# The first cross attention's tiles as steps -16 to -1 of the local layers' pipeline, instead of a stage of its own with a loop

## What is computed

```python
xn = layernorm(x)                                   # 2048 rows of 128
q = xn @ Ly + Lo;  k = ctx @ Lx                     # per head
p = softmax((q @ k.T) / 8 + mask)
x = x + (p @ (ctx @ Tx) + To0) @ Ty + To1           # the first cross attention
y = layernorm(x)
for d in range(6):                                  # the local layers, on y
    y = y + local_attention(shifted(y), Wqkv[d], q_scale[d], k_scale[d]) @ Wo[d]
    y = y + gated_ffn(y, W1[d], W2[d])
x = x + y                                           # then three small cross attentions,
                                                    # an fp8 product and two expert layers
```

## Time and profile before

| | us |
|---|---|
| median of 3 runs | 2523.07 (2520.99 to 2523.55) |
| the profiled execution | 2521.31 |
| its span in the trace | 2519.5 |
| first mask (tile 0), and last mask (tile 15) of the cross stage | 22.27, 223.55 |
| first product of the local layers | 247.79 |
| first softmax of the local layers | 269.98 |
| TensorE busy | 2381.2 (95%) |
| VectorE, ScalarE, GpSimd busy | 1903.0, 1456.6, 1178.6 |

### The profile page before, as it was taken

How to read it: one execution, slowest core, us unless ns; L and a number is a source line. 1 busy time by engine, 2 the same in 40 slices (tenths; PEclk the granted TensorE clock), 3 DMA queues, 4 the chain that set the end, 5 groups by cost and what they waited for, 6 DMA issues and landing times.

```text
span 2519.5 us, 61076 instructions
## 1 busy us (share of the span) xinstructions
PE 2381.2 (95%) x25532; PEld 1440.2 (57%) x25532; DVE 1903.0 (76%) x3472; ACT 1456.6 (58%) x2048; POOL 1178.6 (47%) x867
## 2 busy tenths in 40 slices
PE   6887899999999999999999999988889999999999
PEld 5775556566665666666665666554555555455443
DVE  4765898999999899999999999966866766455222
ACT  2332566666666666666666666653467677566443
POOL 1222776777677767777767776741211111001000
PEclk9998999999999999999999999999899999999999
DMA  3000000000010000000000000002010101120110
GB/s 123 5 4 6 1 2 2 27 10 13 2 35 2 13 18 19 7 7 27 10 8 7 27 10 11 2 1 78 15 33 15 35 12 40 41 82 21 38 50 30
DMA packets 36006, 55.95 MB, mean 22 GB/s; under 512 B 6365, under 2 KB 20710, under 8 KB 35498
## 3 DMA queue, kind: packets, MB, share of 16 engines
q1 hardware_dynamic: 35754, 52.33, 6.6%
HBM read 51.13 MB, written 1.19 MB: 21 GB/s over the span
## 4 chain that ended last, share of the span: by engine, by line
PE 53%; DVE 23%; ACT 11%; issue 9%; POOL 2%; SPq 0%; DMA 0%; DVEq 0%; POOLq 0%; ACTq 0%
PE w L1417 9%; PE w L1407 9%; DVE turned L1057 4%; PE w L766 4%; DVE norm L1064 4%; PE w L791 4%; PE w L779 4%; PE py L804 4%; PE w L519 3%; DVE straight_odd L1052 2%; DVE top L568 2%; PE w L857 2%; ACT sq L1003 2%; ACT sq L994 2%; PE w L1536 2%
## 5 line engine op out<-in xcount | busy, mean ns | idle before, releaser
L593 POOL TENSOR_TENSOR prob<-prob,rden 128x1024 f32<-128x1024 f32 x112 | 213.4, 1905 | 206.3 <-DVE rden L582 206.3
L563 ACT ACTIVATE prob<-logit 128x512 f32<-128x512 f32 x224 | 137.9, 632 | 282.1 <-DVE logit L571 282.1
L1407 PE MATMUL w<-qT,m_fc 128*128 128x512 f32 x544 | 268.7, 606 | 0.4 <-ACT turned L1654 0.4
L1173 POOL TENSOR_TENSOR straight_odd<-straight_odd,turned 128x1024 f32<-128x1024 f32 x96 | 227.5, 2370 | 82.8 <-DVE turned L1057 79.8
L1173 POOL TENSOR_TENSOR straight<-straight,turned 128x1024 f32<-128x1024 f32 x96 | 226.6, 2369 | 43.5 <-DVE turned L1057 43.5
L1057 DVE TENSOR_TENSOR turned<-w,rot 128x512 f32<-128x512 f32 x384 | 245.6, 681 | 0.0
L1167 POOL TENSOR_TENSOR straight_odd<-straight_odd,rnorms 128x1024 f32<-128x1024 f32 x96 | 180.6, 1903 | 116.8 <-DVE rnorms L1078 116.8
L1064 DVE TENSOR_REDUCE norm<-sq 128x16 f32<-128x1024 f32 x192 | 224.3, 1210 | 0.0
L1167 POOL TENSOR_TENSOR straight<-straight,rnorms 128x1024 f32<-128x1024 f32 x96 | 180.6, 1901 | 72.4 <-DVE rnorms L1078 72.4
L766 PE MATMUL w<-b_wqkv,m_proj 128*128 128x512 f32 x384 | 192.0, 623 | 3.3 <-DVE turned L1057 2.0
L791 PE MATMUL w<-b_wqkv,m_proj 128*128 128x512 f32 x384 | 190.3, 618 | 0.0
(11 more groups left out here) (260 smaller groups left out, 5234.2 us busy)
## 6 DMA issues: line engine op xcount, KB each, us to landing
b_wqkv<-gates SPq DMA_DIRECT2D x64, 256.0 KB, 3.6
b_wqkv<-in_b_wqkv SPq DMA_DIRECT2D x18, 512.0 KB, 3.6
ctxT<-in_ctxT SPq DMA_DIRECT2D x64, 64.0 KB, 1.8
b_wo<-in_b_wo SPq DMA_DIRECT2D x6, 512.0 KB, 3.8
m_fc<-in_m_fc SPq DMA_DIRECT2D x1, 2304.0 KB, 8.8
m_proj<-in_m_proj SPq DMA_DIRECT2D x1, 2304.0 KB, 13.0
m_fc<-in_m_fc SPq DMA_DIRECT2D x8, 256.0 KB, 3.2
m_proj<-in_m_proj SPq DMA_DIRECT2D x8, 256.0 KB, 3.7
```

Of the source, the lines that this page charges most:

```text
L593: pool.tensor_tensor(flat, flat, k.rden[:, s, :, None].broadcast_to([P, HEADS, SEQ]), ALU.mult).then_inc(k.prob_ready, 1)
L1173: pool.tensor_tensor(k.straights[s][:, i, :, :], k.straights[s][:, i, :, :], k.turned[:, i, :, :], ALU.add).then_inc(added, 1)
L1407: pe.matmul(claim(("hidden", J, c)), k.m_fc[:, x, c * P:(c + 1) * P], k.m_xT[:, q, :], start=True, stop=True).then_inc(k.ring_full, 1)
```

## The change

The stage cross0 and its loop are gone. Its tiles are steps -16 to -1 of `layers_*`, all unrolled, in the three stages of a local step: step g computes queries and keys of tile g, values and scores of g-1, softmax and attention of g-2, and also the output products of g-3 (`cross_rows`, all eight in one piece, ahead of the softmax's transposes), the update of `k.x` for g-3 and the second normalisation of g-4. `oT` is written in two buffers in turn, so that line 661's successor (`output_bias`) waits for `o_psum` alone. The attention output of the cross tiles goes to `w2` instead of `w0`. The product with the row of ones is gone: GpSimd adds `a_to1`, spread over 128 partitions by its load, to `k.x` (`add_to1`) once the tile has been normalised. The quantisation jobs lie in steps -13 to -10, each on VectorE between the update and `output_bias`; `turn_x` of steps -11 and -10 waits for them, because they share `pt`. The rows are turned into `k.z` in steps -8, -4, 0 and 4.

The core of the diff:

```diff
-        k.a_to1 = sb("a_to1", [1, P])
+        k.a_to1 = sb("a_to1", [P, P])
+QUANTISE = -12
 def stages_of(g):
-    return [0 <= g - n < STEPS for n in range(3)]
+    return [-TILES <= g - n < STEPS for n in range(3)]
+def is_cross(g):
+    return -TILES <= g < 0
 def layers_tensor(pe, k):
+    def turn_x(g):
+        T = FIRST + g
+        pe.wait_ge(k.norm.normed, T + 1)
+        pe.wait_ge(k.xT_ready, T)
...
+        if g - 2 == QUANTISE:
+            pe.wait_ge(k.quant.done, 1)
+        pe.transpose(k.pt[:, 0:P], k.normed[:, g % 2, :], k.ident[:, :]).then_inc(k.xT_psum, 1)
...
+    def cross_scores(g):
+        T = FIRST + g
+        pe.wait_ge(k.qT_ready, T + 1)
+        if is_cross(g + 1):
+            pe.wait_ge(k.kT_ready, T + 2)
+        else:
+            pe.wait_ge(k.kT_ready, T + 1)
+            pe.wait_ge(k.k_turned, T + 2)
+        scores_tensor(pe, k, g % 2)
+    def cross_rows(g):
+        T = FIRST + g
+        pe.wait_ge(k.oT_ready, T + 1)
+        pe.wait_ge(k.updated, T)
+        for h in range(PAIRS):
+            mm = pe.matmul(k.py[:, 0:P], k.oT[:, h, g % 2, :], k.a_ty[:, h, :], start=(h == 0), stop=(h == PAIRS - 1))
+        mm.then_inc(k.y_psum, 1)
...
-    pe.wait_ge(k.quant.done, 1)
-    turn_in(0)
-    for g in range(STEPS + OUTPUT + 1):
+    turn_x(-TILES)
+    pe.wait_ge(k.loaded, 16 * N_URGENT)
+    for g in range(-TILES, STEPS + OUTPUT + 1):
+        if is_cross(g):
+            cross_queries(g)
...
+        if is_cross(g - 1):
+            cross_values(g - 1)
...
+        if is_cross(g):
+            cross_keys(g)
...
+        if is_cross(g - 3):
+            cross_rows(g - 3)
...
+        if is_cross(g + 1) and g >= -TILES:
+            turn_x(g + 1)
...
         if before2:
             turn_probs(g - 2, before)
...
+        if is_cross(g - 1):
+            cross_scores(g - 1)
...
         if before2:
             pe.wait_ge(k.pT_ready, FIRST + g - 1)
             attend_tensor(pe, k, g % 2, k.w2).then_inc(k.o_psum, 1)
 def layers_vector(dve, k):
+    def output_bias(g):
+        dve.wait_ge(k.o_psum, FIRST + g + 1)
+        dve.tensor_tensor(k.oT[:, :, g % 2, :], k.w2[:, :].rearrange("p (h n) -> p h n", n=P),
+                          k.a_to0[:, :, None].broadcast_to([P, PAIRS, P]), ALU.add).then_inc(k.oT_ready, 1)
...
+        if is_cross(g - 2):
+            cross_shift(g - 2)
...
+        if is_cross(g + 2):
+            cross_stats(g + 2)
+        if is_cross(g):
+            query_bias(g)
+        if is_cross(g + 2):
+            cross_normalise(g + 2)
+        if is_cross(g - 4):
+            cross_fresh(g - 4)
+        if before2:
             softmax_sum_vector(dve, k, T - 2, s)
...
+        if is_cross(g - 3):
+            cross_update(g - 3)
...
+        if g == QUANTISE + 1:
+            quantise_weights(dve, k)
+        if g == QUANTISE + 2:
+            fp8_weight_vector(dve, k)
+        if is_cross(g - 2):
+            output_bias(g - 2)
 def layers_gpsimd(pool, k):
+    def add_to1(g):
+        x = k.x[:, g + TILES, :]
+        pool.wait_ge(k.norm.normed, FIRST + g + 1)
+        pool.tensor_tensor(x, x, k.a_to1[:, :], ALU.add).then_inc(k.to1_added, 1)
```

More of the change, by code:

```diff
@@ L372, in _ @@
             gpsimd_program(nc, pool, k)
[L375 to L392, removed]
@@ L397, in cross0_tensor @@
[L397 to L452, removed]
-        if this:
-            pe.wait_ge(k.prob_ready, T + 1)
-            pe.wait_ge(k.v_ready, T + 2 if after else T + 1)
-            for h in range(PAIRS):
-                mm = pe.transpose(k.w2[:, h * P:(h + 1) * P],
-                                  k.prob[:, s, 2 * h:2 * h + 2, :].rearrange("p a m -> p (a m)"), k.ident[:, :])
-            mm.then_inc(k.pT_psum, 1)
-        if before:
-            rows(range(2, 6))
-        if this:
-            wait_apart(pe, k, k.pT_ready, T + 1)
-            pe.wait_ge(k.qT_ready, T + 2 if after else T + 1)
-            attend_tensor(pe, k, s, k.w0).then_inc(k.o_psum, 1)
-        if after2:
-            turn_x(T + 2, s)
-        if before:
-            rows(range(6, PAIRS))
-            pe.matmul(k.py[:, 0:P], k.ones[0:1, :], k.a_to1[0:1, :], start=False, stop=True).then_inc(k.y_psum, 1)
-    turn_x(first, 0)
-    turn_x(first + 1, 1)
-    pe.wait_ge(k.loaded, 16 * N_URGENT)
-    front(first, 0, False)
-    short_steps(pe, first, step)
@@ L935, in layers_tensor @@
             hidden(hid, 0, g)
-        if before:
+        if before and g >= 1:
             turn_queries(g - 1, this)
@@ L989, in layers_scalar @@
         if before2:
-            exp_scalar(act, k, T - 2, s, 8.0)
-        if this:
+            exp_scalar(act, k, T - 2, s, 0.125 if is_cross(g - 2) else 8.0)
+        if this and not is_cross(g):
             act.wait_ge(k.q_psum, T + 1)
@@ L1135, in layers_vector @@
             gate(hid, 0)
-        if this:
+        if local:
             rotate(g, 1, k.w1, k.k_turned, k.k_squared, k.kT_psum, k.k_added)
```

259 lines of the change are left out of this document (128 added, 131 removed).

## The result

The changed kernel takes 2527.72 us (median of 10 runs, 2521.92 to 2530.55) against 2522.82 for the kernel before (10 runs, 2520.99 to 2524.64): ratio 1.0019, 95% interval 1.0010 to 1.0027. It is a little slower, by 4.9 us where 11 were forecast. The same kernel, run again beside experiments, gave 2526.05 (11 runs) against 2522.89, ratio 1.0012 (1.0003 to 1.0021).

A forecast was written before the change was run, and what follows sets the result against it. It took a closed chain of 13.28 us a tile through VectorE, GpSimd, TensorE and ScalarE as the bound. At the full clock -8.2, plus 20 for the falling clock, on 2521.3 gave 2533, median 2534 us; 8-in-10 range 2512 to 2546.

The forecast's parts named there:

- The main case: Cross steps up to the first local softmax: slower by the longer chain and a falling clock, 2534 us, chance 0.57.
- the price of a fall of the clock, "I take 1.9": Transposes, scores and attention on TensorE: a fall to the low clock adds 1.9 us to a step, at most 2.5.
- The first mask: Start of the cross steps: the first softmax mask moves from 22.27 to about 28.7 us.
- The ring: Closed chain from one tile's mask to the next over four engines: 14.16 us instead of 13.28, with 2.24 inserted on VectorE.
- "What the change removes", 1.16: Output bias on VectorE waits for the attention alone: that link is 1.23 instead of 2.39, -1.16 us a tile.
- Fourteen steps at the full clock: Cross steps from the first mask on: 13.9 us for the first and 184.1 for thirteen more.
- The rounding: Rounding of the weights in step -11, for which `turn_x` waits ahead of the transposes: some 2.0 us more.
- The clock: Fourteen cross steps: the clock falls in about three of four, 14 x 0.75 x 1.9 = +20 us, bounds 0 and +35.
- The end of the old stage: The 46 us from the last mask to the first local softmax go away; that softmax comes at 261.9 against 269.98, -8.1.
- the clock holds: Cross steps: the granted clock does not fall, time 2521.3 - 8.2 = 2513 us, faster; chance 0.2.
- The inserted work is not on the ring: Cross steps: the chain is then 11.92 us and the time 2482 us; chance 0.05.
- The rule on the shared port: Rounding in step -11 on VectorE waits for GpSimd's scaling, some 0.9 us once; left out of the sum.

The follow-up runs named there:

- experiment 3: The changed kernel with the query bias alone put behind the softmax sum: 2524.83 us, ratio 1.0008 to the kernel before.
- experiment 4: The changed kernel with only the two normalisations of a step moved behind the softmax sum: 2519.32 us, ratio 0.9990 to the kernel before.
- 5: The changed kernel with both normalisations and the query bias behind the softmax sum, only the statistics ahead: 2500.98 us, ratio 0.9919 to the kernel before.
- experiment 1: The changed kernel with statistics, query bias and both normalisations behind the softmax sum, and GpSimd's root behind its scaling: 2499.14 us, ratio 0.9907 to the kernel before.
- 6: The kernel before with `oT` in two buffers, so the output bias no longer waits for the last output products: 2522.82 us, ratio 0.9995.
- 7: The kernel before with two `oT` buffers and the next tile's scores ahead of the attention: 2514.04 us, ratio 0.9966.
- experiment 10: The changed kernel with TensorE's turning waiting only for the weights' steps to be read, not the whole rounding: 2522.39 us, ratio 0.9999 to the kernel before.
- experiment 2: The changed kernel with each cross tile's output products computed twice over on TensorE: 2518.86 us, ratio 0.9982 to the kernel before.
- 8: The changed kernel with all four inserted operations behind the sum, and the rounding's step read early, TensorE waiting for that alone: 2490.56 us, ratio 0.9869 to the kernel before.

## Why the prediction came out as it did

The main case was right in its direction and its mechanisms: a longer ring, a shorter stage end, and a clock that falls in most steps. It gave 2534; 2527.7 was measured. The step that failed is **the price of a fall of the clock, "I take 1.9"**: it measured 1.21, and the clock took 10.9 us of the fourteen steps instead of 20. Term by term, up to the first local softmax (forecast 281.9 with the clock, measured 271.33 in the profiled execution):

- **The first mask**, "about 28.7": 29.50 in this execution, and 30.22 to 32.17 in the repeat and the eight experiments built on the changed order. Too early by 0.8, and by some 2.5 for a usual run.
- **The ring**, 14.16: 14.05. The sum is right and one of its reasons is not. "Their inputs are ready, so they start at once" is false for the first normalisation, which needs GpSimd's root of the statistics of the same step. The bias hides that wait, and so counts nothing by itself (experiment 3); with the normalisations gone it counts 1.13 (4 and 5). The total of 2.24 came out as 1.92 by experiment 1, as with nothing in front of it the sum starts 3.89 behind the mask and not 3.71.
- **"What the change removes", 1.16**: the ring over VectorE was read rightly, but a second one on TensorE had the same length, and removing that wait alone gives nothing (6). The change gets it because its order also puts the next tile's scores ahead of the attention, which is what 7 does to the old order.
- **Fourteen steps at the full clock**, 198.0 without the rounding: the trace has two at 13.79, ten at 14.05 and two at 13.33, counting every step at what its kind takes when the clock holds: 194.7. Missed: the last two have no statistics and no first normalisation (1.7), step -13, like -14, has no second one (0.4), and the other steps are 0.11 shorter each. -3.3.
- **The rounding**, +2.0: 2.6, the delay of the transposes in step -11; experiment 10 takes all of it away. With the 0.9 of the shared port, which the sum left out, the forecast would have been 2.9. The spreading, put at nothing, delayed step -12 by 0.15, and step -7 started its transposes 0.34 late, which no term of the sum has.
- **Steps 0 and 1**, 33.2: 33.12 (238.21 to 271.33), -0.1.
- **The clock**, "14 x 0.75 x 1.9 = +20": the fourteen steps took 208.7, of which 194.7 and the delays of 3.1 are accounted for: **10.9**, in nine steps. So "three of four", 10.5 steps, was 9, and the price is 1.21 and not 1.9. The prediction had both ends on the page: 2.5 if the clock is low throughout, half of it if it comes back in between. The low stretch covered two of the ring's three TensorE pieces and not all: scores and attention in steps such as -4 (0.69 and 0.79 more), transposes and scores in steps such as -8 (0.88 and 0.68 more). The lower end was the right one. (The window 252:253 of the earlier trace rows lies inside the idle stretch of 2.00 and not behind it; behind it, from 253 to 260, the clock is 1.00 too, so the reading holds.) Rounding and clock together were put at 22.0 and, with the small delays, took 14.0: -8.0.
- **The end of the old stage**: the 46 us from the last mask to the first local softmax, with their idle stretches and the low clock at 263, went away with the old order, as the -8.2 supposed. Behind the first local softmax another 0.7 was gained.

That makes 271.33 against 281.9: +0.8 - 3.3 - 8.0 - 0.1 = -10.6. In the median the gap closes to 6, and that is luck: the profiled execution is the fastest of its ten, and the others are slower than the forecast allowed for. The repeat, 7.2 longer, has a later start and more low-clock time. The forecast took the difference between median and profiled execution over from the kernel before (1.8); it is 5.8 here.

Of the rivals, "the clock holds" was wrong for this kernel. Its 2513 for a clock that does hold is not refuted: the profiled execution less 10.9 is 2511.0 (an estimate), and experiment 2, at 2518.86, holds it in twelve steps of fourteen, begins later (first mask at 31.38) and waits longer in step -11. "The inserted work is not on the ring" fell to experiment 1. The rule on the shared port, +0.9 once, is borne out: in step -11 two operations of the rounding, 0.69 long each in the kernel before (the last one in the earlier trace rows), took 1.47 and 0.88 beside GpSimd, 0.97 more. Both have two inputs in SBUF, as the rule asks; the operation of the earlier trace rows has one, so it does not show that rule. Timeline of VectorE, profile after:

```profile
82.10 1.47 DVE L1201 TENSOR_TENSOR s_w<-s_w,wrstep 128x512 f32<-128x512 f32 x1
...
84.53 0.88 DVE L1205 TENSOR_TENSOR s_w<-s_w,wstep 128x512 f32<-128x512 f32 x1
```

The Trainium skill, "SBUF — State Buffer", section "Who interferes with whom", has VectorE and GpSimd take turns on one port pair; the normalisation of 2.03 in experiment 4 agrees with it too.

**What stays open.** Why the clock held behind 3.01 of idle time in steps -10 and -5 and fell behind 3.00 in step -9 and 2.31 in step -8 was not settled, and neither was how much of the later start in other executions is the loading at the program's start.

## What to carry to other kernels

When one wait on a ring is removed, look for another ring of nearly the same length before booking the gain: read what the *next* instruction waits for, on every engine of the ring. On an engine that works in order, put ahead of the instruction that the ring waits for only what cannot be done later. Here moving four operations behind the sum, and reading a small result early, was worth 35 us, on a change that cost a little as it stood. Two inserted operations don't add up where one of them hides another's wait, so price them together or in both orders. And where a cost lies between a low and a high bound, as a fall of the clock did here, ask how many of the ring's pieces it covers before choosing a value between them.

## What the runs showed of the hardware

- More work on TensorE made the kernel faster: with 1.8 us of repeated products in each step's idle piece the granted clock stayed at 2.4 GHz in twelve of fourteen steps (in five without them), and the time fell by 7 to 9 us (experiment 2).
- The length of the last idle piece did not decide alone. In the changed kernel the clock fell behind pieces of 2.31 to 3.38 us, and held behind others of 2.28 to 3.01. In experiment 4 it held behind 2.03 and 2.04, fell behind 2.19, and did either behind 2.46 to 2.48. In the fourteen steps of experiments 1, 2 and 8 it never fell behind pieces of 0.5 to 1.7.
- A fall cost 1.04 to 1.41 us of a step of 14.05, as it covered two of the three pieces that stand in a row on TensorE; where it covered all three, in experiment 10, it cost 2.24.
- A 128 x 128 operation of VectorE with two inputs in SBUF that starts beside GpSimd's scaling may last until that is over, 2.03 instead of 0.35 (experiment 4).
